# Splitting and stacking k early: VectorE's split of k moved ahead of the seventh score maximum, SyncE's copies of k moved ahead of the shift's rows

## The chip, the cores and the metric

The kernel runs on one core of a Trainium2 chip. The metric is the device time of one launch in microseconds, and the number that counts is the median over several runs. The core has TensorE (PE, matmuls), VectorE (DVE), ScalarE (ACT), GpSimd (POOL) and SyncE (SP). SyncE here only issues DMAs, and the transfers run on 16 DMA engines which all queues of the core share. TensorE's clock is granted in two levels, 2.4 GHz (1.0 in the profile's rows) and 1.2 GHz (0.5).

## What is computed

A layer norm, a cross attention with two key sets, its output projection and residual, then a layer norm and a top-2 mixture of six small feed-forward experts, for 16 samples of 256 tokens and 512 features:

```python
y_dca, y_main = y[:, -DCA:, :], y[:, :-DCA, :]            # 16 and 240 of 256 context rows
q = _ln((x @ Wq + bq).reshape(b, s1, H, HD), qn_w, qn_b)   # 16 heads of 32
k, v = _ln(y_main @ Wk + bk), y_main @ Wv + bv             # per head, 240 keys
k_dca, v_dca = ...                                         # the same with Wkv_dca, 16 keys
ctx = attn(q, k, v) + attn(q, k_dca, v_dca)                # two softmaxes, q k^T / sqrt(32)
x = x + ctx @ Wo + bo
gate_probs = softmax(layernorm(x).mean(axis=1) @ gate_W.T); top 2, renormalised
x = x + sum over the two experts of gate * (gelu(layernorm(x) @ W1 + b1) @ W2 + b2)
```

All of it is in float32 accuracy. The change touches only the attention part, which ends at about 834 us of the profiled span; the feed-forward part takes the rest.

## The kernel before

The attention phase is a software pipeline over the 16 samples, written out by hand: each engine has one program, in which `walk` calls `body` once per step, and a step `b` does the attention of sample b beside the projections of samples b+1 and b+2. The steps are `p0`, `p1`, `p2` (filling), `first` (b = 0), twelve of `body` (b = 1 to 12, a loop of six turns with two steps each), `late` (b = 13), `later` (b = 14), `last` (b = 15) and `tail`. In `late` and `later` parts of the projections are missing, in `last` all of them. The order of the code in `body` is the order on an engine; engines wait for each other only through semaphores.

A step has two halves. In the first, TensorE forms the scores of (token tile, quad of heads) in eight groups (`scores`, L601, into two buffers `sc0` and `sc1` by turns). For each group VectorE takes the maxima (`group_max`: the reduction L925, then L928 and L930) and ScalarE then forms the exponentials and their sums (`exps`, L762). Behind group 3 (exponentials, L777) and group 5 (`dca_sums`, L937), and behind groups 6 and 7, the 16 extra keys get the same. TensorE takes group k+2 only when ScalarE has done group k. Other work stands between the groups: TensorE's projections and transposes, ScalarE's copies of xT (L730).

Between the halves lies the shift. ScalarE takes the logarithm of the sums (`ld`, L812), VectorE forms maximum minus logarithm (`lt`, L1017 and L1019), TensorE transposes it (L610), VectorE splits it in two parts (`s_hi` L1023, `s_lo` L1025), and four small DMAs write the parts as rows of the stacked queries QS (`shift_rows`, L343: `s_hi` from SyncE, `s_lo` from ScalarE's queue). In the second half TensorE forms the scores again, transposed and with the shift in them (`scores_t`, L622), ScalarE takes the exponentials (`probabilities`, L771), and TensorE multiplies with v (`values`, L637). The normalisation of the next q and k runs beside it: `bias_q` (L943), squares on ScalarE (L737), their sums on VectorE (`sum_squares`, L880), the power -1/2 on GpSimd (L452).

Each of q and k of the next sample is needed as a high and a low part (`split_parts`: a copy that rounds, L954, then a subtraction, L956) and stacked in three blocks of partitions (`stack_parts`, L384: 12 DMAs of 128 KB from SyncE for each of QS and KS). Step b makes those of sample b+1, and `scores` of step b+1 waits for all of them (`q_in`, `k_in`). ScalarE makes `kf` (L743) from k's transposes behind group 3 of the same step, and `qf` near the end of the step before. VectorE's order in a step is: groups 0 to 5, first `dca_sums`, groups 6 and 7, second `dca_sums`, split of q, `bias_q` 0, the shift, sum of squares 0, split of k, `bias_q` 1, sum of squares 1 and so on. SyncE's order is: xin, a part of v, store of x2 (L410), load of xres (L413), the two `s_hi` DMAs, q's 12 copies, k's 12 copies, cin (L422). One semaphore `split` counts the four split instructions of a step.

Of the kernel before, what the change touches and what calls it, by code (L numbers as in the profile page):

```python
# [64 lines left out]
def wait(eng, sem, value):  # L65

    if not isinstance(value, int) or value > 0:
        eng.wait_ge(sem, value)
# [92 lines left out]
def attention_phase(nc, stack, early, moe, x, ctx, Wq, bq, Wk, bk, Wv, bv, Wdca, bdca, qn_w, qn_b, kn_w, kn_b,  # L161
# [26 lines left out]
    def sb(name, shape, dt=F32):  # L188
# [3 lines left out]
    wq, wkv, xin, xh, xT, q1, kb, kf, qf, q_hi, q_lo, k_hi, k_lo = (  # L192
        early[n] for n in "wq wkv xin xh xT q1 kb kf qf q_hi q_lo k_hi k_lo".split())
# [17 lines left out]
    QS = [early["QS0"], sb("QS1", [ST, HP, G, S], F32R)]  # L211
    KS = [sb(f"KS{i}", [ST, HP, G, TOK], F32R) for i in range(2)]
# [136 lines left out]
    @block.sync  # L349
    def _(sp):  # L350
        sp.dma_start(xin[:, :, :], x_t[0]).then_inc(x_ld, 16)
        sp.dma_start(wq[:, :, :], Wq.rearrange("(c p) n -> p c n", p=P)).then_inc(wq_ld, 16)
        sp.dma_start(cin[:, :, :], ctx_t[0]).then_inc(c_ld, 16)
        sp.dma_start(wkv[:, :, 0:D], Wk.rearrange("(c p) n -> p c n", p=P)).then_inc(wkv_ld, 16)
        sp.dma_start(wkv[:, :, D:2 * D], Wv.rearrange("(c p) n -> p c n", p=P)).then_inc(wkv_ld, 16)
        for dst, src in ((bq_b[:, :], bq), (bkv_b[:, 0:D], bk), (bkv_b[:, D:2 * D], bv)):
            sp.dma_start(dst, src.partition_broadcast(P)).then_inc(b_ld, 16)
        sp.dma_start(wdca, Wdca.rearrange("(c p) n -> p c n", p=P)).then_inc(wd_ld, 16)
        sp.dma_start(bd_b, bdca.partition_broadcast(P)).then_inc(wd_ld, 16)
        sp.dma_start(wo[:, :, :], Wo.rearrange("(c p) n -> p c n", p=P)).then_inc(wo_ld, 16)  # L360
        sp.dma_start(bo_b[:, :], bo.partition_broadcast(P)).then_inc(wo_ld, 16)

        def store_vdca():

            for c in range(ND):
                wait_evac(sp, "p1", f"DV{c}", -2)
                sp.dma_start(vd_dram[c * BD:(c + 1) * BD].rearrange("b k n -> (b k) n"),
                             vdca[:, c, :]).then_inc(vd_st, 16)
            sp.wait_ge(vd_st, 16 * ND)

        def load_vdca(m, par):

            sp.dma_start(v[par][ROWS[NC - 1]:P, NC - 1, :],
                         vd_dram[m] if isinstance(m, int) else
                         vd_dram[bass.ds(m, 1)].rearrange("b k n -> (b k) n")).then_inc(v_ld[par], 16)

        def stack_parts(m, par, n):

            tensor, hi, lo, order, done = ((QS, q_hi, q_lo, (0, 2, 1), q_in),
                                           (KS, k_hi, k_lo, (0, 1, 2), k_in))[n]  # L380
            sp.wait_ge(split, 4 * m + 2 * n + 2)
            for part, blk in zip((hi, hi, lo), order):
                for h in range(HP):
                    sp.dma_start(tensor[par][blk * HD:(blk + 1) * HD, h, :, :].bitcast(F32),  # L384
                                 part[h * HD:(h + 1) * HD, :, :].bitcast(F32)).then_inc(done, 16)

        def body(step, b, par):
            if step in STATS and step != "p0":
                sp.wait_ge(xh_rdy, T * (b + 3))
                sp.dma_start(xin[:, :, :], x_t[b + 3]).then_inc(x_ld, 16)  # L390
            if step == "p2":
                store_vdca()
            if step == "first":
                for j in range(2):
                    wait_evac(sp, "p1", f"KD{j}", -2)
            if step in KEYED:
                if step in ATTN:
                    wait(sp, ctx_rdy, b)
                load_vdca(b + 1, 1 - par)
            if step == "last":  # L400

                sp.wait_ge(ctx_rdy, B - 1)
                sp.wait_ge(q_in, STACKED * B)
                sp.wait_ge(k_in, STACKED * B)
                moe.load_small(sp)
                for n in range(EARLY_LOADS):
                    moe.load(sp, n)
            if step in WOUT:
                wait_evac(sp, step, "WO1", b)
                sp.dma_start(x2_dram[b - 1], xres[:, :, :]).then_inc(x2_st, 16)  # L410
                sp.wait_ge(x2_st, 16 * b)
            if step in ATTN:
                sp.dma_start(xres[:, :, :], x_t[b]).then_inc(r_ld, 16)  # L413
                sp.wait_ge(sh_hi, b + 1)
                for a in range(2):
                    shift_rows(sp, par, a, s_hi, 0)
            if step in KEYED:
                stack_parts(b + 1, 1 - par, 0)
                stack_parts(b + 1, 1 - par, 1)
            if step in PROJ and step != "late":  # L420
                wait_full(sp, step, "CT", b)
                sp.dma_start(cin[:, :, :], ctx_t[b + 3]).then_inc(c_ld, 16)  # L422
            if step == "last":
                for n in range(EARLY_LOADS, 2 * moe.NE):
                    moe.load(sp, n)

        walk(sp, body)


# [290 lines left out]
    def _(act):  # L720
# [58 lines left out]
        def body(step, b, par):  # L779
# [54 lines left out]
            if attn:  # L834
                probabilities(step, b, 5)
            if proj:
                wait(act, split, 4 * (b + 1) + 2)
                affine_out(step, b, "QT0", qf[:, 0:2, :], affine_q)
                affine_out(step, b, "QT1", qf[:, 2:4, :], affine_q)
            if step == "p1":  # L840
# [13 lines left out]
    def _(dve):  # L854
# [79 lines left out]
        def dca_sums(b, t):  # L934

            dve.wait_ge(d_exp, 2 * b + t + 1)
            dve.tensor_reduce(den[:, t, H:2 * H], ed[:, t, :, :, :].rearrange("p h g n -> p (h g) n"),  # L937
                              AX_X, ALU.add).then_inc(d_den, 1)
# [12 lines left out]
        def split_parts(m, n, whole, hi, lo, stacked):  # L951

            wait(dve, stacked, STACKED * m)
            dve.tensor_copy(hi[:, :, :], whole[:, :, :]).then_inc(split, 1)  # L954
            dve.wait_ge(split, 4 * m + n + 1)
            dve.tensor_tensor(lo[:, :, :], whole[:, :, :], hi[:, :, :].bitcast(F32),  # L956
                              ALU.subtract).then_inc(split, 1)

        def split_q(m):

            split_parts(m, 0, qf, q_hi, q_lo, q_in)

        def split_k(step, b):

            for name in ("KT0", "KT1"):
                wait_evac(dve, step, name, b)
            dve.wait_ge(kd_rdy, b + 2)
            split_parts(b + 1, 2, kf, k_hi, k_lo, k_in)

        def ctx_out(step, b, g):  # L970
            bank = wait_full(dve, step, f"PV{g}", b)
# [10 lines left out]
        def body(step, b, par):  # L982
# [22 lines left out]
            if attn:  # L1005
                group_max(b, 5)
                dca_sums(b, 0)
                group_max(b, 6)
                group_max(b, 7)
                dca_sums(b, 1)  # L1010
# [15 lines left out]
                                  ALU.subtract).then_inc(taken(step, "LT"), 1)  # L1026
            if proj:
                var(0)
            if keyed:
                split_k(step, b)  # L1030
            if proj:
                bias_q(step, b, 1)
                var(1)
# [502 lines left out]
```

## Time and profile before

| | us |
|---|---|
| time of three runs | 1194.06 (1193.3 to 1195.92) |
| the profiled execution: its own time | 1188.21 |
| its span | 1186.4 |
| TensorE busy | 960.7 |
| VectorE busy | 812.4 |
| ScalarE busy | 636.6 |
| GpSimd busy | 294.3 |

The span is the time between the first and the last instruction of the profiled execution. Its mean granted clock was 0.938 of 2.4 GHz. Busy times are sums over the whole span; a step of the attention part takes about 45 us of it, and which engine sets its end changes within a step.

### The profile page before, as it was taken

To read this page: it belongs to the slowest core of one execution; us is meant where nothing else is said; L and a number is where in the kernel's file an instruction comes from. 1 tells how busy PE (TensorE), PEld (TensorE's weight loads), DVE (VectorE), ACT (ScalarE), POOL (GpSimd) and SP (SyncE) were. 2 spreads that over 40 slices of the span, in tenths; PEclk is the share of its full clock that TensorE was granted. 3 is DMA by queue.
4 is the path that set the end of the run, shared out by engine and by line. 5 is a ranking of instruction groups with operands and counts; after the bars stand their busy time and mean duration, and the time that the engine had idled before them with its cause. 6 is when DMAs were issued, how large, how long until landed. Compare 5 with 4: busy or idle time off the path is not lost. (4 is left out here: it accounts for less than half of the span.)

```text
span 1186.4 us, 17325 instructions
## 1 busy us (share of the span) xinstructions
PE 960.7 (81%) x5020; PEld 647.3 (55%) x5020; DVE 812.4 (68%) x1706; ACT 636.6 (54%) x1658; POOL 294.3 (25%) x203
## 2 busy tenths in 40 slices
PE   1767888888888889798788888556379999999998
PEld 0335444445445445445445445333368888888887
DVE  5446777767768777777777775551767777777775
ACT  0227677677677677776775776654433131313131
POOL 0492522513514514404415324000000000000000
PEclk9886999999999999999999999687589999999999
DMA  7132543534624624615525424476201111111100
GB/s 248 42 92 64 138 104 104 137 89 116 138 71 118 152 59 115 150 60 131 139 67 136 121 68 111 105 227 197 89 36 54 53 53 53 52 54 49 56 36 36
DMA packets 56406, 116.31 MB, mean 98 GB/s; under 512 B 13945, under 2 KB 22393, under 8 KB 56121
## 3 DMA queue, kind: packets, MB, share of 16 engines
q1 hardware_dynamic: 53760, 115.16, 35.5%
q10 hardware_dynamic: 2616, 0.79, 0.3%
q8 instruction: 14, 0.23, 0.1%
q14 instruction: 16, 0.12, 0.0%
HBM read 47.24 MB, written 17.30 MB: 54 GB/s over the span
## 5 line engine op out<-in xcount | busy, mean ns | idle before, releaser
L452 POOL TENSOR_TENSOR vs<-vs,neg_half 128x16 f32<-128x16 f32 x66 | 199.9, 3058 | 460.6 <-DVE vs L882 460.0
L762 ACT ACTIVATE sc<-sc,nm 128x240 f32<-128x240 f32 x512 | 225.0, 457 | 98.9 <-DVE ed L930 98.8
L925 DVE TENSOR_REDUCE pm<-sc 128x64 f32<-128x1024 f32 x128 | 156.1, 1219 | 31.6 <-PE sc L601 30.4
L771 ACT ACTIVATE pt<-sc 128x1024 f32<-128x1024 f32 x128 | 125.3, 1020 | 81.6 <-PE sc L622 81.6
L1348 ACT ACTIVATE hb<-hb 128x352 f32<-128x352 f32 x64 | 31.9, 498 | 227.8 <-DVE hb L1404 227.8
L554 PE MATMUL ring<-wq,xT 128*128 128x512 f32 x256 | 133.9, 672 | 16.0 <-ACT xT L730 16.0
L601 PE MATMUL sc<-KS,QS 96*128 96x256 f32 x512 | 104.7, 335 | 46.1 <-ACT sc L762 41.6
L601 PEld LDWEIGHTS sc<-KS,QS 96*128 96x128 f32 x512 | 74.8, 202 | 86.2 <-ACT sc L762 60.6
L567 PE MATMUL ring<-wkv,cT 128*128 128x512 f32 (+1 forms) x256 | 121.0, 607 | 0.0
L762 ACT ACTIVATION_READ_ACCUMULATOR sc<-sc,nm 128x1 f32 x512 | 118.0, 230 | 0.0
L646 PE MATMUL ring<-wo,ot 128*128 128x512 f32 x256 | 116.2, 597 | 0.6 <-DVE ot L972 0.6
L622 PE MATMUL sc<-QS,KS 100*128 100x256 f32 x512 | 89.9, 320 | 26.9 <-DMA QS<-s_lo 26.3
L622 PEld LDWEIGHTS sc<-QS,KS 100*128 100x128 f32 x512 | 70.7, 199 | 56.2 <-issue 40.2
L554 PEld LDWEIGHTS ring<-wq,xT 128*128 128x128 f32 x256 | 52.8, 217 | 76.0 <-issue 63.7
L1224 PE MATMUL f_ring<-w_hi,f_xT_hi 128*128 x256 | 85.2, 333 | 2.6 <-DVE f_xT_lo L1386 2.6
L1224 PE MATMUL f_ring<-w_hi,f_xT_lo 128*128 x256 | 84.6, 330 | 0.0
L1224 PE MATMUL f_ring<-w_lo,f_xT_hi 128*128 x256 | 84.3, 329 | 0.0
L637 PE MATMUL ring<-pt,v 128*32 128x256 f32 x1024 | 70.3, 392 | 16.2 <-ACT pt L771 16.2
L880 DVE TENSOR_REDUCE vs<-sq 128x16 f32<-128x512 f32 x66 | 45.0, 682 | 53.7 <-ACT sq L737 52.8
L1280 PE MATMUL f_ring<-w_hi,hT_hi 128*128 (+1 forms) x192 | 79.0, 412 | 0.0
L1280 PE MATMUL f_ring<-w_lo,hT_hi 128*128 (+1 forms) x192 | 76.3, 397 | 0.0
L1280 PE MATMUL f_ring<-w_hi,hT_lo 128*128 (+1 forms) x192 | 75.9, 395 | 0.0
(137 smaller groups left out, 1652.6 us busy)
## 6 DMA issues: line engine op xcount, KB each, us to landing
QS<-q_hi SPq DMA_DIRECT2D x128, 128.0 KB, 3.0
KS<-k_hi SPq DMA_DIRECT2D x128, 128.0 KB, 3.0
xin<-in_x_dram SPq DMA_DIRECT2D x16, 512.0 KB, 4.0
QS<-q_lo SPq DMA_DIRECT2D x64, 128.0 KB, 3.0
KS<-k_lo SPq DMA_DIRECT2D x64, 128.0 KB, 2.9
xres<-in_x_dram SPq DMA_DIRECT2D x16, 512.0 KB, 3.2
x_scratch<-xres SPq DMA_DIRECT2D x16, 512.0 KB, 2.6
x<-x_scratch SPq DMA_DIRECT2D x16, 512.0 KB, 3.2
```

The source lines that it names most:

```text
L452: pool.tensor_tensor(w, w, neg_half[0:rows, :], ALU.pow).then_inc(rstd, 1)
L554: last = pe.matmul(bank[:, :], xT[:, kc, t * P:(t + 1) * P], wq[:, kc, :], start=(kc == 0), stop=(kc == KC - 1))
L567: last = pe.matmul(bank[0:ROWS[c], :], cT[:, cc, c * P:c * P + ROWS[c]], kv_half(wkv[:, cc, :], half), start=(cc == 0), stop=(cc == CC - 1))
L601: last = pe.matmul(sc[k % 2][:, i // 2, (i % 2) * TOK:(i % 2 + 1) * TOK], QS[par][0:BLK, i, quad, t * P:(t + 1) * P], KS[par][0:BLK, i, qu ...
L622: last = pe.matmul(sc[p % 2][:, i, c * S:(c + 1) * S], KS[par][:, h, g, c * P:(c + 1) * P], QS[par][:, h, g, :], start=True, stop=True)
L637: last = pe.matmul(bank[i * HD:(i + 1) * HD, 0:S], v[par][:, c, h * HD:(h + 1) * HD], pt[g % 2][:, i, c * S:(c + 1) * S], start=(c == 0), ...
L646: last = pe.matmul(bank[:, :], ot[:, g, t * P:(t + 1) * P], wo[:, g, :], start=(g == 0), stop=(g == G - 1))
L762: last = act.activation(s, s, ACT.Exp, bias=nm[:, t, h:h + 1], accum_out=den[:, t, h:h + 1])
L771: act.activation(pt[g % 2][:, (p % 2) * 2:(p % 2) * 2 + 2, :], sc[p % 2][:, :, :], ACT.Exp).then_inc(sc_evac[p % 2], 1)
L925: dve.tensor_reduce(pieces, s.rearrange("p h (c n) -> p h c n", n=DCA), AX_X, ALU.max, negate=True).then_inc(g_max, 1)
L1224: last = pe.matmul(bank[:, 0:FF], xT[xp][:, kc, t * P:(t + 1) * P], w1[wp][:, bass.ds(ex[e], 1), kc, :].rearrange("p a f -> p (a f)"), sta ...
L1280: last = pe.matmul(bank[:, :], hT[hp][0:rows, e, fc, t * P:(t + 1) * P], w2[wp][0:rows, bass.ds(ex[e], 1), fc, :].rearrange("p a n -> p (a ...
```

## The change

In a step VectorE splits k behind the first `dca_sums`, ahead of the maxima of groups 6 and 7, and no longer behind the shift. Since k's split now comes before q's, k has the numbers 1 and 2 of the four counts of `split` and q has 3 and 4; ScalarE's wait ahead of the next `qf` goes with that. SyncE issues k's 12 copies behind the load of xres, ahead of its wait for the shift's rows; q's 12 copies stay behind these rows. In step `p2`, where there is no attention yet, k's split and copies also come ahead of q's.

```diff
         def stack_parts(m, par, n):
-            tensor, hi, lo, order, done = ((QS, q_hi, q_lo, (0, 2, 1), q_in),
-                                           (KS, k_hi, k_lo, (0, 1, 2), k_in))[n]
+            tensor, hi, lo, order, done = ((KS, k_hi, k_lo, (0, 1, 2), k_in),
+                                           (QS, q_hi, q_lo, (0, 2, 1), q_in))[n]
             sp.wait_ge(split, 4 * m + 2 * n + 2)
...
                 sp.dma_start(xres[:, :, :], x_t[b]).then_inc(r_ld, 16)
+            if step in KEYED:
+                stack_parts(b + 1, 1 - par, 0)
+            if step in ATTN:
                 sp.wait_ge(sh_hi, b + 1)
                 for a in range(2):
                     shift_rows(sp, par, a, s_hi, 0)
             if step in KEYED:
-                stack_parts(b + 1, 1 - par, 0)
                 stack_parts(b + 1, 1 - par, 1)
...
-                wait(act, split, 4 * (b + 1) + 2)
+                wait(act, split, 4 * (b + 1) + 4)
...
-            split_parts(m, 0, qf, q_hi, q_lo, q_in)
+            split_parts(m, 2, qf, q_hi, q_lo, q_in)
...
-            split_parts(b + 1, 2, kf, k_hi, k_lo, k_in)
+            split_parts(b + 1, 0, kf, k_hi, k_lo, k_in)
...
                 group_max(b, 5)
                 dca_sums(b, 0)
+            if keyed:
+                split_k(step, b)
+            if attn:
                 group_max(b, 6)
                 group_max(b, 7)
                 dca_sums(b, 1)
...
                 var(0)
-            if keyed:
-                split_k(step, b)
             if proj:
                 bias_q(step, b, 1)
```

How this stands in the programs of the engines is shown for one step of the loop (line numbers of the changed kernel are 2 higher on most of these lines). First VectorE from the first `dca_sums` (`den<-ed`) on, before:

```order
L937 TENSOR_REDUCE den<-ed 128x16
L922 REGISTER_ALU
L925 TENSOR_REDUCE pm<-sc 128x4x16
L927 REGISTER_ALU
L928 TENSOR_REDUCE nm<-pm 128x4
L930 TENSOR_TENSOR ed<-sc,pm 128x4x16
L925 TENSOR_REDUCE pm<-sc 128x4x16
```

and in the changed kernel from the same place:

```order
L939 TENSOR_REDUCE den<-ed 128x16
L297 REGISTER_ALU
L969 REGISTER_ALU
L68 REGISTER_ALU
L956 CAST k_hi<-kf 128x1024
L957 REGISTER_ALU
L958 TENSOR_TENSOR k_lo<-kf,k_hi 128x1024
L924 REGISTER_ALU
L927 TENSOR_REDUCE pm<-sc 128x4x16
L929 REGISTER_ALU
L930 TENSOR_REDUCE nm<-pm 128x4
L932 TENSOR_TENSOR ed<-sc,pm 128x4x16
```

The two large instructions on k now stand between the sum of the extra keys and the maxima of group 6; everything of groups 6 and 7 is queued behind them. The place that they leave is behind the shift, between the first sum of squares (`vs<-sq`) and `bias_q` 1 (`q<-ring`), before:

```order
L880 TENSOR_REDUCE vs<-sq 128x16
L881 ISA
L882 TENSOR_SCALAR vs<-vs 128x16
L297 REGISTER_ALU
L954 CAST k_hi<-kf 128x1024
L955 REGISTER_ALU
L956 TENSOR_TENSOR k_lo<-kf,k_hi 128x1024
L943 TENSOR_TENSOR q<-ring,bq_b 128x512
```

and in the changed kernel:

```order
L882 TENSOR_REDUCE vs<-sq 128x16
L883 ISA
L884 TENSOR_SCALAR vs<-vs 128x16
L945 TENSOR_TENSOR q<-ring,bq_b 128x512
L880 REGISTER_ALU
L882 TENSOR_REDUCE vs<-sq 128x16
```

Here `bias_q` 1 follows the sum at once. Last SyncE from the load of xres to the end of the burst of copies, before:

```order
L413 DMA xres<-in_x_dram 128x2x512
L343 DMA QS<-s_hi 1x16x256 x2
L381 ISA
L384 DMA QS<-q_hi 32x1024 x8
L384 DMA QS<-q_lo 32x1024 x4
L381 REGISTER_ALU
L384 DMA KS<-k_hi 32x1024 x8
L384 DMA KS<-k_lo 32x1024 x4
```

and in the changed kernel:

```order
L413 DMA xres<-in_x_dram 128x2x512
L381 ISA
L384 DMA KS<-k_hi 32x1024 x8
L384 DMA KS<-k_lo 32x1024 x4
L343 DMA QS<-s_hi 1x16x256 x2
L381 REGISTER_ALU
L384 DMA QS<-q_hi 32x1024 x8
L384 DMA QS<-q_lo 32x1024 x4
```

k's twelve issues moved from the end of the burst to its front, past the two issues of the shift's rows.

## Rows read from the trace of the kernel before

**Rows 1.** Waits: who waited for whom, us in total, times, longest us.

```profile
ACT sc L762 <- DVE ed L930: 98.8, 37, 7.0
```

**Rows 2.** VectorE's timeline, step 7: start, us, operation [idle before <-releaser].

```profile
429.92 0.41 DVE L937 TENSOR_REDUCE den<-ed 128x16 f32<-128x256 f32 x1
430.86 1.23 DVE L925 TENSOR_REDUCE pm<-sc 128x64 f32<-128x1024 f32 x1 [0.53 <-PE sc L601]
...
432.25 0.21 DVE L930 TENSOR_TENSOR ed<-sc,pm 128x64 f32<-128x64 f32 x1
...
434.99 0.42 DVE L937 TENSOR_REDUCE den<-ed 128x16 f32<-128x256 f32 x1 [0.65 <-ACT ed L777]
435.33 0.68 DVE L954 CAST q_hi<-qf 128x1024 fp32r<-128x1024 f32 x1
...
438.39 0.19 DVE L1017 TENSOR_TENSOR lt<-nm,ld 128x32 f32<-128x32 f32 x1 [0.52 <-ACT ld L812]
```

**Rows 3.** ScalarE's timeline, the same stretch.

```profile
432.75 0.46 ACT L762 ACTIVATE sc<-sc,nm 128x240 f32<-128x240 f32 x1
...
434.49 0.47 ACT L777 ACTIVATE ed<-ed 128x256 f32<-128x256 f32 x1
```

**Rows 4.** VectorE's timeline behind the shift, step 7.

```profile
441.73 0.69 DVE L954 CAST k_hi<-kf 128x1024 fp32r<-128x1024 f32 x1
...
443.60 0.68 DVE L943 TENSOR_TENSOR q<-ring,bq_b 128x512 f32<-128x512 f32 x1
447.13 0.69 DVE L880 TENSOR_REDUCE vs<-sq 128x16 f32<-128x512 f32 x1 [2.84 <-ACT sq L737]
```

**Rows 5.** TensorE's timeline around the shift, step 7.

```profile
436.54 0.60 PE L543 MATMUL ring<-ident,cin 128*128 128x128 f32 x4
438.75 0.39 PE L610 MATMUL ring<-ident,lt 128*32 128x128 f32 x2 [1.61 <-DVE lt L1019]
438.98 3.60 PE L554 MATMUL ring<-wq,xT 128*128 128x512 f32 x8
443.87 1.21 PE L622 MATMUL sc<-QS,KS 100*128 100x256 f32 x8 [1.29 <-DMA QS<-s_lo]
```

**Rows 6.** ScalarE and VectorE at the shift of step 8.

```profile
479.61 0.47 ACT L777 ACTIVATE ed<-ed 128x256 f32<-128x256 f32 x1
484.16 0.18 DVE L1017 TENSOR_TENSOR lt<-nm,ld 128x32 f32<-128x32 f32 x1
```

**Rows 7.** VectorE, ScalarE and TensorE at the shift of step 9.

```profile
521.11 0.41 DVE L937 TENSOR_REDUCE den<-ed 128x16 f32<-128x256 f32 x1
524.22 4.90 PE L554 MATMUL ring<-wq,xT 128*128 128x512 f32 x8
525.96 0.42 ACT L777 ACTIVATE ed<-ed 128x256 f32<-128x256 f32 x1
529.80 0.19 DVE L1017 TENSOR_TENSOR lt<-nm,ld 128x32 f32<-128x32 f32 x1
```

**Rows 8.** SyncE's DMA issues, step 7.

```profile
431.46 0.38 SPq L413 DMA_DIRECT2D xres<-in_x_dram  x1
439.62 1.17 SPq L343 DMA_DIRECT2D QS<-s_hi  x2
```

**Rows 9.** DMA issues of the whole launch: KB each, median us from issue to landing.

```profile
KS<-k_lo SPq DMA_DIRECT2D x64, 128.0 KB, 2.9
QS<-s_hi SPq DMA_DIRECT2D x32, 16.0 KB, 2.6
```

**Rows 10.** TensorE's timeline from step 14 into step 15.

```profile
773.95 1.07 PE L637 MATMUL ring<-pt,v 128*32 128x256 f32 x16 [0.49 <-ACT pt L771]
778.44 1.37 PE L601 MATMUL sc<-KS,QS 96*128 96x256 f32 x8 [3.42 <-issue]
```

**Rows 11.** ScalarE's `kf` and SyncE's last issues in step p2.

```profile
72.37 1.39 ACT L743 ACTIVATE kf<-ring,affine 128x480 f32<-128x480 f32 x2
...
87.97 2.50 SPq L384 DMA_DIRECT2D KS<-k_lo  x4
```

## The prediction

> **What bounds the kernel now.** I read the waits first. ScalarE's exponentials of the first half wait for VectorE's maxima, 98.8 us in all [rows 1]; so the place to which k's split moves lies in front of somebody who waits. Then I read the timelines of one loop step (step 7, whose shift is near 438 us) engine by engine. Behind the first `dca_sums` VectorE takes the maxima of group 6 after 0.53 us of idling, and the second sum waits 0.65 us for ScalarE's exponentials of the extra keys; the first `lt` waits 0.52 us for ScalarE's logarithm [rows 2]. So up to the shift the chain is: VectorE's maxima of group 6, ScalarE's exponentials 6, those of the extra keys, exponentials 7, logarithm, `lt`. From `lt` it goes to TensorE's transposes, which had waited 1.61 us for it, to VectorE's `s_hi` and `s_lo`, through the DMAs, and to the transposed scores, which wait 1.29 us for the rows of `s_lo` [rows 5]. Behind the shift ScalarE's exponentials and squares hold the chain: VectorE stands idle 2.84 us before the sum of squares 1, waiting for ScalarE's square [rows 4]. The reader should see there that the place which k's split leaves is followed by idle time larger than the split, and that the place to which it goes is not.
>
> **Ahead of the maxima (added).** From k's rounding copy to the operation behind its subtraction 443.60 - 441.73 = 1.87 us pass [rows 4]. A `dca_sums` holds VectorE 435.33 - 434.99 = 0.34 us [rows 2]. In step 7 the split therefore stands from 429.92 + 0.34 = 430.26 to 432.13. The maxima of group 6 began at 430.86 and now begin at 432.13, 1.27 us later. The last operation of the group begins 432.25 - 430.86 = 1.39 us behind the first and takes 0.21 [rows 2], so ScalarE can begin exponentials 6 at 433.73. It began them at 432.75, when its copies of xT were done [rows 3]: 0.98 us later. These copies are all the cover there is. Group 7 follows at 432.13 + 1.39 + 0.13 = 433.65 (the 0.13 an estimate for the last operation's place in the pipeline) and is done by 435.2, ahead of 434.49 + 0.98 = 435.47, where the exponentials of the extra keys now start, so it adds nothing. The logarithm and `lt` come 0.98 us later in such a step. No wait for k's inputs is new: ScalarE made `kf` behind group 3.
>
> How much of the 0.98 reaches `lt` differs by step. From the start of the second exponentials of the extra keys to `lt` step 7 takes 438.39 - 434.49 = 3.90 us; four of the thirteen steps 1 to 13 are like this: 4 x 0.98 = 3.9. In step 8 it takes 484.16 - 479.61 = 4.55 [rows 6]: there TensorE's projection Q0 was late and `bias_q` 0 held VectorE, so 0.65 of the delay is covered and 0.33 is left; four steps: 1.3. Two lie between (4.29 and 4.38 us, 0.59 and 0.50 left): 1.1. In step 9 Q0 took 4.90 us and the last scores came late too: 525.96 - 521.11 = 4.85 us from the first sum to those exponentials instead of 434.49 - 429.92 = 4.57, so the new 4.57 + 0.98 = 5.55 is 0.70 later; its `lt` follows after 3.84 us and covers nothing [rows 7]. Three steps: 2.1. Step 0 had its scores of group 6 late by more than the split: 0. Sum for steps 1 to 13: 8.4 us.
>
> **Behind the shift (removed).** The 1.87 us go from in front of an idle stretch of 2.84 us [rows 4]; it grows to 4.7, since ScalarE's square 1 comes behind its exponentials 0 and 1, which come behind the shift's rows. What is late next is the same thing as before. Bounds: 0, and a gain of 1.87 x 13 = 24 us if VectorE were what the second half waits for there. I take 0, since the idle row is at this very place in the loop.
>
> **SyncE's queue (moved).** Twelve issues take 12 x 2.50 / 4 = 7.5 us [rows 11]. SyncE is free behind xres at 431.84 [rows 8], starts k's at about 432.2 when the split is done, and is through at 439.7. The wait for `s_hi` ends at 439.62 + 0.98 = 440.6: 0.9 us of margin. The transfers behind the last issue land 2.9 us after it, the small rows 2.6 after theirs [rows 9]: k's last at about 439.1 + 2.9 = 442.0, the first `s_hi` at 443.2. So the shift's rows are hardly touched, and what PE waits for is `s_lo`, which is issued later and on ScalarE's queue. Bounds: 0, and 0.9 us a step if a stall of SyncE eats the margin twice over; I take 0. The Trainium skill has a rule against the change here: "DMA: Bandwidth & Descriptors", section "Queues, rings and completion order", says that descriptors of one queue are consumed in ring order on each engine, while engines take turns between queues. By that rule `s_hi`, on SyncE's queue, would stand behind what is left of k's copies, and `s_lo` would not; with the landings just worked out it costs nothing unless k's burst is late, which is the second rival below.
>
> q's copies keep their place behind the rows and the stack is complete 7.5 us sooner after the shift. Who waits for that? At the start of step 15 TensorE is through with the values at 773.95 + 1.07 = 775.02 and begins the scores at 778.44; the 3.42 us before them [rows 10] I read as the wait for k's last copies (nothing else of theirs is open). With k gone from the end of the burst it vanishes, except that the whole step 14 comes 0.70 later (its rows are like those of step 9): 3.42 - 0.70 = 2.7 us gained once. In steps 1 to 14 the scores follow the values without idling, so nothing is gained. The skill speaks for the change as well: the same page, section "Rules for kernel authors", says to issue a DMA early and wait on it late, which hides its cost. The trace has only this one place where it would.
>
> In `p2` k's split now waits for `kf`, ready at 72.37 + 1.39 = 73.76, and is done near 75.7; 24 issues of 0.63 us end at 90.8 instead of 87.97 + 2.50 = 90.47 [rows 11], and the first scores wait for them: 0.4 us (bounds 0 and 1).
>
> **TensorE's clock.** The gap before the `lt` transposes grows from 438.75 - 437.14 = 1.6 us to 2.6 in steps like 7 [rows 5]. The trace has no row for such a gap. From one side it costs 0. From the other: in step 9 a fall of the clock to 1.2 GHz, after gaps in the scores 6 and 7, stretched Q0 to 4.90 us [rows 7], against 3.60 for Q1 at 2.4 GHz [rows 5]; 1.30 us on Q1 would just use up the 1.29 us before the transposed scores; a fall of its whole length would cost 3.60 - 1.29 = 2.3 us a step, 30 us over 13 steps. A fall that runs into the transposed scores costs some tenths. I take the nearest row with a little over it: 1 us in all.
>
> **Sum.** 8.4 - 2.7 + 0.4 + 1.0 = 7.1 us. The profiled execution would go from 1188.21 to 1195.3. The median of the runs was 5.85 us above that execution; I keep this distance: 1194.06 + 7.1 = 1201.2 us.
>
> **Rivals.**
> (a) The clock falls in most steps behind the longer gap: 0.5 to 0.8 us for each of 13 steps, 8.5 more than the 1.0 taken: 1209.7. For it: gaps of about 1 and 1.2 us ahead of the scores 6 and 7 already bring falls in about nine of sixteen steps. Against it: Q1 has 1.29 us in hand, and where Q0 is slow the gap stays near 0.9. 0.14.
> (b) SyncE is late with the shift's rows, because k's burst starts behind a late xres or one issue stalls: more than 0.9 us of lateness must come first, and `s_lo` hides 0.5 more. At 0.6 us in 13 steps: 1209. 0.08.
> (c) On the other side: k's copies out of the way is worth more than the delay. The mechanism is that VectorE's lateness at group 6 is covered, because ScalarE reaches exponentials 6 late anyway, as behind the slow Q0. It decides once ScalarE comes to them more than 1 us later than now. Then steps 1 to 13 cost 0, and the sum is 0.4 - 2.7 = -2.3: 1191.8. For it: part of the delay is covered in six of thirteen steps already. Against it: 98.8 us of ScalarE waiting for these maxima [rows 1]. 0.10.
> The forecast itself has 0.68. That order and semaphores do something else than said I give nothing: the orders show the move.
>
> **Numbers.** This kernel's runs tell no change from one below 0.2%, 2.4 us. The forecast's own range is 1197 to 1206. For 8 in 10, with the uncertain distance between median and profile and part of (a) and (b), 1195.5 to 1208. Slower by over 0.2%: 0.68 of the forecast nearly whole, and (a) and (b): 0.86. Within: 0.07 from both sides. Faster: most of (c), 0.07.
>
> **What the profile after would show.** VectorE: k's split directly behind the first `dca_sums`, no idling before group 6, and `lt` 8.47 + 0.98 = 9.45 us behind that sum in nearly every step, with the 0.5 us wait for the logarithm in nearly all. ScalarE: about 1 us of idling before exponentials 6, with VectorE as the releaser. VectorE before the sum of squares 1: 4.7 us of idling. SyncE: `s_hi` issued at once when ready. TensorE: no wait before the scores of step 15, and loop steps of 46.2 us instead of 45.6. I am wrong if exponentials 6 start as early as before, if the gap before the transposed scores shrinks, or if the second half of a step gets shorter without k's 1.87 us in it.

## The result, and the profile after

The changed kernel takes 1210.08 us (median of four runs, 1207.23 to 1211.57) against 1193.68 us for the kernel before beside it: a ratio of 1.0131, interval 1.0100 to 1.0161. It is slower, as forecast, but by 16.4 us where 7.1 were forecast, and 1210.1 lies outside the range of 1195.5 to 1208. The profiled execution took 1208.91 us over a span of 1207.1; the span of before was 1186.4.

To see where the 20.7 us of span went, I took for each step the start of its first maxima (`g0`), of its first `dca_sums` (`d0`), of `lt`, and of the transposed scores (`sT`) from the timelines of VectorE and TensorE:

| from the traces, us | before | changed | difference |
|---|---|---|---|
| launch to `g0` of step 0 | 93.65 | 100.40 | +6.75 |
| steps 0 to 13 | 639.41 | 654.65 | +15.24 |
| step 14 | 46.13 | 43.99 | -2.14 |
| `g0` of step 15 to the end | 407.21 | 408.06 | +0.85 |
| of steps 1 to 12, mean: `d0` to `lt` | 8.82 | 9.55 | +0.73 |
| `lt` to `sT` | 5.45 | 5.60 | +0.15 |
| `sT` to the next `g0` | 16.23 | 16.49 | +0.26 |

The place that I had argued from looks as forecast. This is VectorE's timeline of the changed kernel in step 3 (start, us, operation, in brackets the idle time before it and its releaser), which answers to [rows 2, 4]:

```profile
257.11 0.41 DVE L939 TENSOR_REDUCE den<-ed 128x16 f32<-128x256 f32 x1
257.43 0.68 DVE L956 CAST k_hi<-kf 128x1024 fp32r<-128x1024 f32 x1
258.15 1.22 DVE L958 TENSOR_TENSOR k_lo<-kf,k_hi 128x1024 fp32r<-128x1024 f32 x1
259.29 1.22 DVE L927 TENSOR_REDUCE pm<-sc 128x64 f32<-128x1024 f32 x1
...
266.54 0.19 DVE L1022 TENSOR_TENSOR lt<-nm,ld 128x32 f32<-128x32 f32 x1 [0.22 <-ACT ld L814]
...
270.77 0.69 DVE L945 TENSOR_TENSOR q<-ring,bq_b 128x512 f32<-128x512 f32 x1 [0.91 <-PE ring L556]
275.51 0.69 DVE L882 TENSOR_REDUCE vs<-sq 128x16 f32<-128x512 f32 x1 [4.05 <-ACT sq L739]
```

No idle time is left before group 6; `lt` comes 266.54 - 257.11 = 9.43 us behind the first sum (9.45 forecast); and where the split had been VectorE now waits, 0.91 us before `bias_q` 1 and 4.05 us before the sum of squares 1 (4.7 us were forecast, all before the sum), so nothing was gained there. ScalarE in the same step now waits before exponentials 6, as it did not in [rows 3]:

```profile
260.93 0.44 ACT L764 ACTIVATE sc<-sc,nm 128x240 f32<-128x240 f32 x1 [0.84 <-DVE ed L932]
```

In the waits over the launch (us in total, times, longest us) this group went from 98.8 us [rows 1] to

```profile
ACT sc L764 <- DVE ed L932: 110.9, 50, 6.2
```

What I had not seen is in step `p2`. VectorE of the changed kernel, first k's split of the launch, then the first maxima:

```profile
79.95 0.69 DVE L956 CAST k_hi<-kf 128x1024 fp32r<-128x1024 f32 x1 [13.36 <-POOL kf L459]
...
100.40 1.23 DVE L927 TENSOR_REDUCE pm<-sc 128x64 f32<-128x1024 f32 x1 [5.47 <-PE sc L603]
```

The split waits 13.36 us, not for ScalarE's part of `kf`, which was ready at 73.9, but for GpSimd, which copies the 16 extra keys into it. GpSimd's timeline of the kernel before, which the prediction does not show, had this to be read:

```profile
64.63 15.24 POOL L446 MEMSET KS<- 4x3840 f32 x8
79.94 0.24 POOL L457 COPY kf<-kdT 128x64 f32<-128x64 f32 x1
```

The copy (`dca_keys`) stands behind eight memsets of the constant rows of KS, 15.24 us in a row. Before, k's split came at 80.99 and the copy was done. Now q's split and 24 DMA issues stand behind it.

In the loop two further things cost. First, the shift's rows land late. This is TensorE in step 11 and the DMA issues between 639.4 and 643 us (KB each, median us from issue to landing), both of the changed kernel; compare [rows 5, 9]:

```profile
645.01 1.21 PE L624 MATMUL sc<-QS,KS 100*128 100x256 f32 x8 [1.60 <-DMA QS<-s_lo]
646.06 3.25 PE L569 MATMUL ring<-wkv,cT 128*128 128x512 f32 x4
```

```profile
KS<-k_lo SPq DMA_DIRECT2D x1, 128.0 KB, 3.2
QS<-s_hi SPq DMA_DIRECT2D x2, 16.0 KB, 3.0
QS<-s_lo ACTq DMA_DIRECT2D x2, 16.0 KB, 3.4
```

SyncE's last four issues for k end at 639.87 and those of `s_hi` begin at 640.45, so k's last copies, which take 3.2 us to land, are still under way when the rows are issued. The rows of `s_hi` land after 3.0 us instead of 2.6, and those of `s_lo` after 3.4 instead of 2.8, although they go through ScalarE's queue. Second, the projection behind the transposed scores takes 3.25 us there. The same instructions take 1.88 us in step 3. The windows of these microseconds show why (length in us; busy us of PE, its weight loads, VectorE, ScalarE and GpSimd with counts; then TensorE's granted clock, DMA share and GB/s):

```profile
645.00:647.00 2.00, 1.99 (x10) 1.59 (x11) 0.00 (x0) 1.22 (x2) 0.52 (x1) 0.86 1.00 205
647.00:649.00 2.00, 2.00 (x4) 0.68 (x2) 0.69 (x2) 1.24 (x2) 0.00 (x0) 0.50 1.04 209
```

The clock fell to 1.2 GHz behind the wait of 1.60 us. Such a fall behind the shift occurred in steps 1 and 11, and both times `sT` to the next `g0` took 17.7 us, where the odd steps without one take 16.0. The length of the wait does not decide it: in step 9 it was 1.70 us, and no fall came. At groups 6 and 7 this profile has twelve falls in steps 1 to 13 where that of before has nine. Ten of them are as long as before and leave `lt` at 9.43 us; those of steps 4 and 7 are of double length, and `lt` comes there at 10.1 us.

The start of step 15 is as forecast. TensorE goes from the values to the scores without the 3.42 us of [rows 10]:

```profile
797.26 1.07 PE L639 MATMUL ring<-pt,v 128*32 128x256 f32 x16 [0.65 <-ACT pt L773]
798.26 1.22 PE L603 MATMUL sc<-KS,QS 96*128 96x256 f32 x8
```

### The profile page after: what moved, and what is told of

Same layout as the page of the kernel before. It is cut to its first block and busy times, and to the rows that moved or that the text cites. A ratio compares the mean times of both kernels' runs of the same rounds, so it can differ in the third digit from the quotient of the medians.

```text
span 1207.1 us, 17325 instructions
## 1 busy us (share of the span) xinstructions
PE 971.2 (80%) x5020; PEld 650.9 (54%) x5020; DVE 808.5 (67%) x1706; ACT 637.8 (53%) x1658; POOL 287.9 (24%) x203
## 5 line engine op out<-in xcount | busy, mean ns | idle before, releaser
L454 POOL TENSOR_TENSOR vs<-vs,neg_half 128x16 f32<-128x16 f32 x66 | 192.3, 2940 | 489.0 <-DVE vs L884 488.5
L764 ACT ACTIVATE sc<-sc,nm 128x240 f32<-128x240 f32 x512 | 224.5, 452 | 111.0 <-DVE ed L932 110.9
L556 PE MATMUL ring<-wq,xT 128*128 128x512 f32 x256 | 141.1, 703 | 15.5 <-ACT xT L732 15.3
L569 PE MATMUL ring<-wkv,cT 128*128 128x512 f32 (+1 forms) x256 | 124.5, 621 | 0.1
L603 PEld LDWEIGHTS sc<-KS,QS 96*128 96x128 f32 x512 | 73.9, 199 | 86.9 <-ACT sc L764 62.0
L764 ACT ACTIVATION_READ_ACCUMULATOR sc<-sc,nm 128x1 f32 x512 | 114.8, 224 | 0.0
L556 PEld LDWEIGHTS ring<-wq,xT 128*128 128x128 f32 x256 | 55.7, 229 | 79.7 <-issue 67.3
```

The lines of the kernel that those rows point to most:

```text
L454: pool.tensor_tensor(w, w, neg_half[0:rows, :], ALU.pow).then_inc(rstd, 1)
L556: last = pe.matmul(bank[:, :], xT[:, kc, t * P:(t + 1) * P], wq[:, kc, :], start=(kc == 0), stop=(kc == KC - 1))
L569: last = pe.matmul(bank[0:ROWS[c], :], cT[:, cc, c * P:c * P + ROWS[c]], kv_half(wkv[:, cc, :], half), start=(cc == 0), stop=(cc == CC - 1))
L603: last = pe.matmul(sc[k % 2][:, i // 2, (i % 2) * TOK:(i % 2 + 1) * TOK], QS[par][0:BLK, i, quad, t * P:(t + 1) * P], KS[par][0:BLK, i, qu ...
L764: last = act.activation(s, s, ACT.Exp, bias=nm[:, t, h:h + 1], accum_out=den[:, t, h:h + 1])
```

## The experiments

Each ratio is to the kernel before, run in turns with it on the same chip, with its 95% interval. The medians of before were 1190.91, 1192.62 and 1192.38 us in the three groups of runs; single runs of it spread from 1186.6 to 1197.6, which is more than most effects here, so I read the parts from the traces and only the sums from the times. In most of these kernels a list of steps, `KFIRST`, says where k comes first; the counts of `split` and the order in `stack_parts` follow it. The cuts show only the lines that move work.

**Step p2 left alone.** The changed kernel; in `p2` q is split and stacked first as before. Against the changed kernel:

```diff
+    KFIRST = ('first', 'body', 'late', 'later')
...
-            if keyed:
+            if keyed and step in KFIRST:
                 split_k(step, b)
...
+            if keyed and step not in KFIRST:
+                split_k(step, b)
```

> The changed kernel, with the old order in step p2 alone (q's split and copies first, k's behind). Theory: of the 20.7 us that the profiled execution lost, 6.7 are lost before the first scores, because in p2 VectorE waits at k's split for GpSimd's copy of the extra keys into kf. Then this kernel is 6.3 to 6.8 us faster than the changed one (about 1203.5 us), and its first maxima come at about 93.7 us as before. Rival: the start is hidden by something later (a transfer, the loop's own wait), and the time stays within 2 us of the changed kernel's 1210.

Measured: 1203.32 us, ratio 1.0115 (1.0090 to 1.0139). The start is that of before:

```profile
93.88 1.23 DVE L931 TENSOR_REDUCE pm<-sc 128x64 f32<-128x1024 f32 x1 [1.74 <-PE sc L607]
```

The first maxima come 6.5 us earlier than in the changed kernel, so that much at the start belongs to `p2`. The times do not show it by themselves: the ratio is 0.16% below the changed kernel's 1.0131, where 6.5 us would be 0.54%, and the two intervals overlap. That nothing later hides the gain rests on the run with the memsets moved.

**The rows first.** The changed kernel; SyncE issues the shift's rows before k's copies. Against the changed kernel:

```diff
-            if step in KEYED:
-                stack_parts(b + 1, 1 - par, 0)
-            if step in ATTN:
                 sp.wait_ge(sh_hi, b + 1)
                 for a in range(2):
                     shift_rows(sp, par, a, s_hi, 0)
             if step in KEYED:
-                stack_parts(b + 1, 1 - par, 1)
+                stack_parts(step, b + 1, 1 - par, 0)
+                stack_parts(step, b + 1, 1 - par, 1)
```

> The changed kernel with VectorE's order untouched, but SyncE issues the shift's rows first, then k's copies, then q's. Theory: the tail of k's copies on the DMA engines delays the shift's rows by 0.3 to 0.4 us in most steps (5.45 us from lt to the transposed scores become 5.7 to 5.9). Then here it is 5.4 to 5.5 in every step, there are no clock falls behind the shift, and the loop steps are about 0.4 us shorter (steps 1 to 13: 5 us less than changed); but the 3.4 us wait at step 15 comes back, so the time is near 1208 us. Rival: the rows are late for another reason (ScalarE's queue, the parity of the loop), then they stay at 5.7 to 5.9 in odd steps and the time is 1212 or more.

Measured: 1206.96 us, ratio 1.0126 (1.0106 to 1.0147). `lt` to `sT` is 5.40 to 5.51 us in every step from 1 to 13, mean 5.45 as before; TensorE in step 11:

```profile
644.32 1.21 PE L624 MATMUL sc<-QS,KS 100*128 100x256 f32 x8 [1.32 <-DMA QS<-s_lo]
```

No fall behind the shift occurred in the loop, and the mean of `sT` to the next `g0` is 16.20. So it was the tail of k's copies that held the rows up. Loop steps took 46.34 us instead of 46.79, and step 14 took 45.98, so that what the change gains there is gone with k's place in the queue. The first maxima came at 103.6 us in this execution; the first `bias_q` of the launch was already 2.3 us later than in the changed kernel's profile, so most of that arose ahead of everything that the edit touches.

**Step later alone.** The kernel before, with the change in step 14 only. Against the kernel before:

```diff
+    KFIRST = ('later',)
...
                 dca_sums(b, 0)
+            if keyed and step in KFIRST:
+                split_k(step, b)
+            if attn:
                 group_max(b, 6)
...
-            if keyed:
+            if keyed and step not in KFIRST:
                 split_k(step, b)
```

> The kernel before, with the change made in step later (b = 14) alone. Theory: k's copies at the end of the burst hold up the scores of step 15 by 3.4 us, and putting them first takes that away at a price of 0.7 us at the shift: step 14 takes 44.0 instead of 46.1 us, and the launch 2 us less than before (1191.7 us). Rival: what is gained there is lost again in step 15 to the clock or to the loads of the experts' weights, and the time equals that of before (1193.7).

Measured: 1190.87 us, ratio 0.9990 (0.9973 to 1.0006). Step 14 takes 44.10 us as expected, and the stretch from step 15 to the end 408.07 instead of 407.21. So 2.0 us are gained in step 14. The 0.9 us more behind it are not shown to come from the edit: two of the kernels below leave step 14 as it was and have 408.8 and 409.1 us there. The ratio does not tell 2 us from nothing, so the times show neither reading. Its loop is that of the kernel before, and is a second sample of it. It has three double falls, a mean of 9.04 us from `d0` to `lt`, and 596.7 us for steps 1 to 13 where the profile of before had 592.8.

**Behind group 7.** k's split behind the maxima of groups 6 and 7; the rows first; `p2` as before. On VectorE, against the changed kernel:

```diff
                 dca_sums(b, 0)
-            if keyed:
-                split_k(step, b)
-            if attn:
                 group_max(b, 6)
                 group_max(b, 7)
+            if keyed and step in KFIRST:
+                split_k(step, b)
+            if attn:
                 dca_sums(b, 1)
```

> k's split ahead of the shift, but behind the maxima of group 7 instead of ahead of those of group 6; SyncE issues the rows first, then k's copies, then q's; p2 as before. Theory: what costs is ScalarE waiting for the maxima of group 6 and not the 1.87 us on VectorE: behind group 7 the split uses the 0.65 us for which VectorE waits there and the 0.5 us before lt, so lt is late by about 0.5 us in steps whose Q0 is in time and by 0 where it is late. Loop steps of 45.8 to 45.9 us, time 1196 to 1197.5. Rival: every 1.87 us put on VectorE ahead of the shift costs about the same 1 us: lt 9.4 us behind the first sum, loop steps of 46.4, time 1203 or more.

Measured: 1200.18 us, ratio 1.0074 (1.0056 to 1.0093); loop steps of 46.15 us. That is between the two readings. Where Q0 is in time (steps 9 and 13) the theory holds: `lt` comes 9.0 us behind the first sum, 0.55 late. It also holds in steps 2, 4, 6 and 10, where the fall came late enough to slow only Q0: `lt` comes at 9.13, as in the kernel before behind such a Q0, so the split is covered. In steps 1, 3 and 5 it is 9.47 to 9.50, where the kernel before had 8.7 to 8.8 in like steps. There the clock had fallen earlier and the scores 7 came late, and VectorE did them, the split, the second sum, q's split and `bias_q` 0 without a pause. This is VectorE in step 3:

```profile
253.47 1.23 DVE L927 TENSOR_REDUCE pm<-sc 128x64 f32<-128x1024 f32 x1 [0.76 <-PE sc L603]
...
256.88 0.41 DVE L939 TENSOR_REDUCE den<-ed 128x16 f32<-128x256 f32 x1
...
259.07 0.68 DVE L945 TENSOR_TENSOR q<-ring,bq_b 128x512 f32<-128x512 f32 x1
259.67 0.18 DVE L1022 TENSOR_TENSOR lt<-nm,ld 128x32 f32<-128x32 f32 x1
```

I had counted on every slow Q0 as cover. It is none where the fall that slows Q0 makes the scores 7 late as well. Two more things add to the time: double falls in steps 7 and 11 (`lt` at 10.2 and 10.1), and a step 14 of 47.45 us where the kernel before has 46.13.

**The changed kernel again**, unchanged, beside the next three.

> The changed kernel once more, to stand beside the next three on one chip. First maxima at 100.4 us, lt 9.4 us behind the first sum in most loop steps, transposed scores 5.4 to 5.9 us behind lt; a time 1.3 to 1.4% above before.

Measured: 1207.29 us, ratio 1.0119 (1.0093 to 1.0145), a little less than expected. First maxima at 104.28 us, not 100.4; the first `bias_q` of the launch was 3.0 us later than in the first profile. Thirteen falls at groups 6 and 7 in steps 1 to 13. Three falls behind the shift (steps 1, 2 and 7), two double ones (steps 3 and 12).

**The memsets out of the way.** The changed kernel with GpSimd's memsets of KS at the end of `p0`.

```diff
+            if step == "p0":
+                pool.wait_ge(const, 5)
+                pool.wait_ge(ln_rs, 2)
+                selectors()
+                pool.wait_ge(ones, 8)
...
-                pool.wait_ge(rstd, T + NC + ND)
-                selectors()
```

> The changed kernel, with GpSimd's eight memsets of the constant rows of KS (14.8 us in all) moved from the end of step p1 to the end of step p0, where GpSimd is idle. Theory: in p2 VectorE's split of k waits until 80 us only because GpSimd's copy of the extra keys into kf stands behind these memsets; with them gone it starts when ScalarE's kf is done, at about 74 us, and the first maxima come at 94 instead of 100.4 us: 6 to 6.5 us less than the changed kernel. Rival: the wait is for ScalarE's kf or for the transposes of the extra keys, then the first maxima stay near 100.

Measured: 1200.28 us, ratio 1.0073 (1.0046 to 1.0100), 7.0 us less than the changed kernel beside it. GpSimd makes its copy at 69.72 us, and VectorE's split of k follows ScalarE's `kf`. VectorE's timeline, then the first maxima:

```profile
75.11 0.69 DVE L963 CAST k_hi<-kf 128x1024 fp32r<-128x1024 f32 x1 [7.25 <-ACT kf L752]
...
95.48 1.23 DVE L934 TENSOR_REDUCE pm<-sc 128x64 f32<-128x1024 f32 x1 [2.69 <-PE sc L610]
```

This settles the cause: the order in `p2` costs 6 to 7 us only because GpSimd's copy stands behind the memsets. Counted from the first `bias_q` of the launch, which the order in `p2` does not touch, the first maxima come after 59.8 us in the kernel before, 59.9 with `p2` left alone and 60.3 with the memsets moved, but after 66.5, 67.3 and 67.3 in the changed kernel, the rows first and the changed kernel again.

**Transposes in the gap.** The changed kernel with TensorE's context transposes between the scores 6 and 7.

```diff
                 scores(b, par, 6)
+            if proj and attn:
+                context_transposes(step, b)
+            if attn:
                 scores(b, par, 7)
             if proj:
                 project_q(step, b, 0)
+            if proj and not attn:
                 context_transposes(step, b)
```

> The changed kernel, with TensorE's context transposes (0.6 us) moved from behind the projection Q0 into the gap between the scores of groups 6 and 7. Theory: the falls of TensorE's clock at groups 6 and 7 come from the idle time there (0.96 and 1.15 us); filling half of the second makes them rarer than the 13 of the profile of the changed kernel's loop, and the double falls, which put Q0 wholly at 1.2 GHz and lt at 10.1 us, go away. As lt is set by ScalarE at 9.4 us otherwise, this gives only the excess back: 1 to 4 us less than the changed kernel. Rival: the falls have nothing to do with this gap; same count, same time.

Measured: 1206.11 us, ratio 1.0115 (1.0085 to 1.0146), not to be told from the changed kernel's 1.0119. The double falls are gone and those at groups 6 and 7 are six in steps 1 to 13, where the two profiles of the changed kernel have twelve and thirteen, as the theory has it. But the gap ahead of the `lt` transposes is now 3.0 us in steps whose Q0 is in time (2.6 without the move). Seven loop steps have such a gap, and in three of them, steps 1, 4 and 9, the clock fell behind it; step 11 has a fall behind the shift. TensorE in step 1, and two windows (columns as above):

```profile
171.24 0.39 PE L616 MATMUL ring<-ident,lt 128*32 128x128 f32 x2 [3.02 <-DVE lt L1032]
171.46 5.30 PE L560 MATMUL ring<-wq,xT 128*128 128x512 f32 x8
176.96 1.21 PE L628 MATMUL sc<-QS,KS 100*128 100x256 f32 x8 [0.20 <-DMA QS<-s_lo]
```

```profile
170.00:172.00 2.00, 0.77 (x4) 0.49 (x5) 0.99 (x4) 1.97 (x3) 0.00 (x0) 0.96 1.03 219
172.00:174.00 2.00, 2.00 (x4) 0.94 (x3) 1.17 (x3) 1.26 (x3) 0.00 (x0) 0.50 0.52 107
```

That is the mechanism of my rival (a), here with a gap of 3.02 us. Q1 took 5.30 us instead of 3.60 and used up nearly all of the wait before the transposed scores, so that `lt` to `sT` grew to 6.09 us in step 1 and not at all in step 4 (5.43).

**A combined version.** The runs pointed at what holds `lt` up in the kernel before, a slow Q0 with `bias_q` 0 behind it, and at the end of step 14. This version has k first in `later` alone, `bias_q` 0 on VectorE behind `lt`, `s_hi` and `s_lo`, ScalarE's square 0 behind its issue of the rows, and the transposes in the gap. k's split, which stays behind the shift in the other steps, comes there ahead of the sum of squares 0 and no longer behind it. Without the transposes, against the kernel before:

```diff
-                sq_unit(0)
             if attn:
                 wait_evac(act, step, "LT", b)
                 for a in range(2):
                     shift_rows(act, par, a, s_lo, 1)
+            if proj:
+                sq_unit(0)
...
-            if proj:
-                bias_q(step, b, 0)
...
             if proj:
+                bias_q(step, b, 0)
+            if keyed and attn and step not in KFIRST:
+                split_k(step, b)
+            if proj:
                 var(0)
```

> The kernel before with three small changes: k first in step later alone; bias_q 0 on VectorE behind the shift instead of ahead of lt (ScalarE issues the rows of s_lo ahead of the square 0); context transposes between the scores 6 and 7. If a late Q0 holds lt up only through bias_q 0 and the transposes behind it, lt comes 8.5 us behind the first sum in nearly every loop step (mean before 8.8 to 9.0), which with step 14 gives 6 to 8 us less than before (0.993 to 0.995 of it). Rival: TensorE itself reaches the lt transposes late after a slow Q0, then nothing but the step 14 part is gained: 0.998.

Measured: 1184.44 us, ratio 0.9933 (0.9910 to 0.9956): 8.2 us less than the kernel before. `d0` to `lt` is 8.46 to 8.65 us in all steps from 1 to 13, and loop steps take 45.32 us. VectorE in step 9, where Q0 again ran at 1.2 GHz for a part (4.96 us):

```profile
526.32 1.23 DVE L968 TENSOR_TENSOR q_lo<-qf,q_hi 128x1024 fp32r<-128x1024 f32 x1
528.65 0.19 DVE L1030 TENSOR_TENSOR lt<-nm,ld 128x32 f32<-128x32 f32 x1 [1.11 <-ACT ld L822]
```

`lt` waits for ScalarE's logarithm and for nothing else.

**Its parts.** `bias_q` 0 behind the shift, alone on the kernel before (with the moves of the square 0 and of k's split that go with it, although the expectation says "nothing else"):

> The kernel before with bias_q 0 behind the shift on VectorE and the rows of s_lo ahead of the square 0 on ScalarE, nothing else. If bias_q 0 is what holds lt up after a slow Q0, lt comes 8.5 us behind the first sum; but TensorE still has Q0 and the context transposes ahead of the lt transposes, so part of it is only moved. Expected 0.996 to 0.998 of before. Rival: all of it is moved and nothing gained (1.000).

Measured: 1189.12 us, ratio 0.9969 (0.9950 to 0.9988), `d0` to `lt` 8.51 us on the mean, as expected. The transposes in the gap, alone:

> The kernel before with TensorE's context transposes between the scores 6 and 7, nothing else. Fewer and shorter falls of the clock at groups 6 and 7 (7 to 8 in the loop instead of 9 to 10, no double ones): 1 to 3 us less than before, 0.998 to 0.999. Rival: the gap has no part in the falls, 1.000, or the transposes delay the scores 7, 1.001.

Measured: 1187.92 us, ratio 0.9968 (0.9951 to 0.9985), `d0` to `lt` 8.68 us, and four falls in steps 1 to 13, where the two profiles of the old order have nine and ten. Seven to eight falls and 1 to 3 us were expected; it is 4.5 us. Each part is worth about 0.3%. The combined version with the memsets moved as well:

> The combined version with GpSimd's memsets of KS moved to the end of step p0 as well. In the order of before, k's split in p2 hardly waits for GpSimd's copy, so the launch start gains little: first maxima at 93 to 95 us, the time within 1 us of the combined version's (0.9925 to 0.994 of before). Rival: the memsets then slow VectorE's centring of the weights in p0 and the start is 1 to 2 us later.

Measured: 1183.89 us, ratio 0.9931 (0.9907 to 0.9955), first maxima at 94.96 us; not to be told from the version without.

## Why the prediction was wrong

**The sign and the main term held.** k's split ahead of group 6 delays `lt` to 9.43 us behind the first sum, as worked out (9.45), in most loop steps of four profiles. That was worked out from the waits and is no luck. I had 8.4 us for steps 1 to 13 against the one profile of before; against that profile the changed kernel's lost 9.6 us, 1.4 of them in the two double falls. Over the four profiles with this order in the loop (changed, changed again, `p2` left alone, memsets moved) the mean from `d0` to `lt` in steps 1 to 12 is 9.52 us, over the two with the old order (before, later alone) 8.93: 0.59 x 13 = 7.7 us. The 0 taken for the place behind the shift held as well: from `sT` to the next `g0` most steps without a fall there take 16.0 us (odd) or 16.4 us (even) in both orders.

**The step that failed is the one on `p2`**: "No wait for k's inputs is new: ScalarE made `kf` behind group 3", and the 0.4 us with bounds of 0 and 1 that came of it. For the loop it is true. In `p2` `split_k` also waits for `kd_rdy`, GpSimd's copy, and I looked at ScalarE's row of `kf` [rows 11] and not at GpSimd's. The term measures 6.75 us between the two profiles and 7.0 us between the two medians with and without the memsets in the way. With the memsets moved, the start costs 0.5 us more than before, counted from the first `bias_q`: the 0.4 was right for the wait that I had looked at. With 6.5 in its place the sum would have been 13 us and the time 1207, inside the range; the 3 us that remain are of the size of the next two terms.

**SyncE's queue was mis-sized.** I took 0 for k's copies ahead of the rows, and the trace says 0.16 us a step from `lt` to `sT` (5.60 on the mean of the four profiles against 5.44), 2.1 us in 13 steps. I had compared when k's last copy and the first `s_hi` land, 442.0 against 443.2, and concluded that they do not meet. But the rows are short transfers which meet the tail of the burst while they are still on their way: from 639.4 to 641.4, behind `lt` of step 11, the DMA share is 0.90, and in the same stretch of step 7 of the kernel before it is 0.00 (changed, then before; columns as above):

```profile
639.40:641.40 2.00, 1.82 (x6) 0.99 (x7) 0.94 (x4) 1.99 (x3) 0.00 (x0) 1.00 0.90 191
438.00:440.00 2.00, 1.25 (x5) 0.76 (x6) 1.09 (x4) 1.96 (x4) 0.00 (x0) 1.00 0.00 0
```

I had also held `s_lo` safe on ScalarE's queue. It landed up to 0.7 us late (3.5 us in step 9), in the same steps as `s_hi`. Neither queue's order explains that, since `s_lo` has no copy of k ahead of it in its own; the 16 engines, busy at a share of 0.97 and 0.90 in the four microseconds from 637.4, are what both have in common. In "DMA: Bandwidth & Descriptors", section "Issuing engines are not separate DMA queues", the Trainium skill says that transfers started by different engines end up on the same 16 DMA engines and interleave. The trace agrees (2.8 to 3.4 us for `s_lo`), and that is the rule which I should have weighed beside the one on ring order.

**The clock term was small but right in kind.** I took 1 us, and some tenths for a fall that runs into the transposed scores. Falls behind the shift, 1.6 to 1.7 us each, came in 2, 3, 0 and 1 of the loop steps of the four profiles. There was none in the loops of before, later alone, rows first and behind group 7, but one each in `bias_q` alone and in the combined version with the memsets moved, whose loops keep the old order of the copies, so k's copies make them likelier at most; that they do is not shown. From `sT` to the next `g0` the four profiles have 16.42 us against 16.22: 0.20 x 13 = 2.6 us. No fall followed the gap that I named, the one before the `lt` transposes, in these four. It was 2.6 to 2.7 us long in only five loop steps of the four profiles, and the clock stayed at 2.4 GHz behind it. The gap stayed shorter elsewhere because Q0 was slow: at groups 6 and 7 the four profiles have 12, 13, 11 and 11 falls in steps 1 to 13, the two of the old order 9 and 10. Falls came only where the gap was 3.0 us long, in three of seven such steps of the kernel with the transposes moved.

**Step 14 held**, with 2.1 us measured for 2.7, and rival (c) fell: ScalarE's wait for the maxima grew from 98.8 to 110.9 us, and `lt` was never earlier than 9.42 us behind the first sum in the loop.

The loop steps came out at 46.79 us where 46.2 were forecast, by the rows, the falls behind the shift and the double ones.

Together, 6.8 at the start, 7.7 to `lt`, 2.1 to the rows, 2.6 behind them and -2.1 in step 14 make 17.1 us, for 16.4 (14.7 in the second group) in the medians. The start and step 14 are each read from one pair of profiles, so that the sum fits this closely is in part luck. The distance of 5.85 us between the profiled execution of before and its median is also explained in part: that profile had nine single falls in its loop, the second sample ten with three of them double, and 3.9 us more for the same steps.

## What to carry to other kernels

When an instruction moves ahead in one engine's program, list every semaphore that it waits for, once for each kind of step in which it occurs, and read in the trace when each was last released: in the filling steps of a pipeline an engine that is idle in the loop may be 15 us behind. A burst of copies placed ahead of a small transfer on which an engine waits can cost that engine something (here 0.16 us a step) even if the burst has been issued in time and the small one goes through another queue. And an edit that gives idle time of one engine for work is only free where the next engine in the chain was itself late; here it was late by the 0.3 us of a copy, and 1.3 us were put in front of it.

## What the runs showed of the hardware

The same program gave different numbers of clock falls from one execution to the next, and what a fall cost depended on where it lay. At groups 6 and 7 of a loop step one lasted about 3.4 us. In the order of before it delayed `lt` by up to 0.7 us when it covered a part of Q0 and by 1.7 when it was of double length (10.17 us behind the first sum in place of 8.47); in the changed order a single one there delayed `lt` by nothing, since `lt` was held at 9.43 us anyway. Behind the shift one cost 1.6 to 1.7. The unchanged kernel's time spreads over 1186.6 to 1197.6 us, and its mean granted clock goes with it: 0.942 in the execution of 1186.6 and 0.930 in that of 1197.6. The clock is not shown to be all of it, since the first `bias_q` of a launch also came anywhere from 33.6 to 37.0 us in the profiles of these kernels. Filling 0.45 us of TensorE's idle time between the scores 6 and 7 (1.15 to 0.70 us) with the transposes left four falls in the loop of the kernel before, by one profile, where two profiles without it have nine and ten.
